# Experts' scatters that add into a row per token, on one core: the shared result is stored first, and the last stage loads one row per token

## The reference, cut to what matters

```python
ys = _geglu(xf @ Ws1 + bs1) @ Ws2 + bs2
logits = (xf @ Wr + br) / TAU
top_val, top_idx = jax.lax.top_k(logits, 2)
top_w = jax.nn.softmax(top_val, axis=-1)
...
yE = jnp.einsum('enh,ehd->end', act, We2) + be2[:, None, :]
yr = jnp.einsum('end,ne->nd', yE, w)
return (ys + yr).reshape(B, T, Dm)
...
x = x + _layernorm(_L0_ffn_ref(_layernorm(x, axis=-1), ...), axis=-1)
```

## Time and profile before

| what | value |
|---|---|
| median of 3 runs | 1189.19 us (1187.93 to 1189.62) |
| span of the profiled execution (its own time is given as this span alone) | 1189.8 us |
| PE, PEld busy over the span | 87%, 50% |
| DVE, ACT, POOL busy over the span | 70%, 63%, 53% |
| granted TensorE clock, mean | 0.957 |

### The profile page before, as it was taken

One profiled execution on the slowest core, in us unless ns is written; L12 is line 12 of the kernel. 1 busy time (PEld: TensorE's weight loads), 2 busy tenths in 40 slices (PEclk: granted clock), 3 DMA queues, 4 the chain that ended last, 5 costly groups with the idle time before them and its releaser, 6 DMA issues. The chain is left out here.

```text
span 1189.8 us, 31490 instructions
## 1 busy us (share of the span) xinstructions
PE 1035.2 (87%) x8446; PEld 597.5 (50%) x8446; DVE 833.9 (70%) x2411; ACT 746.2 (63%) x1311; POOL 631.6 (53%) x1184
## 2 busy tenths in 40 slices
PE   4689998898899898998777999866999999999875
PEld 3543333333333333332245665535888888888732
DVE  7587777777777777776768898532666666666737
ACT  4677767777767767775655566413666666666716
POOL 3246666666666666664422777771444444444344
PEclk9799999999999999998996899878999999999988
DMA  8313333333332333333243111112222222221166
GB/s 222 86 56 97 94 94 94 105 92 90 90 107 86 97 93 100 94 98 104 81 127 130 54 55 55 55 55 71 65 60 62 64 61 64 64 65 51 46 220 211
DMA packets 135606, 107.47 MB, mean 90 GB/s; under 512 B 32203, under 2 KB 127874, under 8 KB 135538
## 3 DMA queue, kind: packets, MB, share of 16 engines
q1 hardware_dynamic: 124722, 87.45, 26.1%
q0 software_dynamic: 8544, 17.78, 4.2%
q10 hardware_dynamic: 2272, 1.45, 0.4%
HBM read 55.96 MB, written 50.69 MB: 90 GB/s over the span
## 5 line engine op out<-in xcount | busy, mean ns | idle before, releaser
L1536 DVE TENSOR_REDUCE maxima<-ps 128x8 f32<-128x1024 f32 x320 | 384.3, 1222 | 125.4 <-PE ps L1159 111.1
L911 ACT ACTIVATE pT_area<-ps 128x1024 f32<-128x1024 f32 x320 | 327.7, 1026 | 143.6 <-PE ps L1190 143.0
L699 POOL TENSOR_SCALAR_AFFINE_SELECT pT_area<-pT_area 128x256 f32<-128x256 f32 (+1 forms) x448 | 190.8, 440 | 109.3 <-ACT pT_area L911 107.4
L801 POOL DMA_INDIRECT ys_dram<-quad_area,place_cur x139 | 133.1, 957 | 192.5 <-issue 136.6
L1231 PE MATMUL ps<-pT_area,quad_area 128*32 128x512 f32 (+3 forms) x2048 | 190.6, 446 | 0.0
L791 POOL DMA_INDIRECT xs_dram<-quad_area,idx_cur x128 | 123.0, 961 | 77.6 <-issue 75.2
L1190 PE MATMUL ps<-quad_area 64*128 64x512 bf16 (+3 forms) x1024 | 124.9, 301 | 37.3 <-DVE maxima L1536 34.7
L1398 PE MATMUL ps<-quad_area 128*128 128x256 f32 (+1 forms) x456 | 129.8, 367 | 6.3 <-issue 4.5
L1399 PE MATMUL ps<-quad_area 128*128 128x256 f32 (+1 forms) x456 | 128.3, 363 | 0.0
L1159 PE MATMUL ps<-quad_area 61*128 61x128 bf16 (+2 forms) x1792 | 126.4, 243 | 0.0
L1019 ACT ACTIVATE xnT<-ps,be_cur 128x256 f32<-128x256 f32 (+1 forms) x228 | 94.6, 448 | 47.6 <-PE ps L1399 47.3
(11 more groups left out here) (237 smaller groups left out, 1593.0 us busy)
## 6 DMA issues: line engine op xcount, KB each, us to landing
qk_dram<-split_area SPq DMA_DIRECT2D x192, 128.0 KB, 2.3
quad_area<-qk_dram SPq DMA_DIRECT2D x256, 96.0 KB, 2.3
row_area<-xs_dram SPq DMA_DIRECT2D x63, 132.0 KB, 2.1
pT_area<-ys_dram SPq DMA_DIRECT2D x16, 512.0 KB, 5.3
pT_area<-in_L_ffn_We SPq DMA_DIRECT2D x12, 384.0 KB, 6.1
out_dram<-pT_area SPq DMA_DIRECT2D x7, 512.0 KB, 2.9
xs_dram<-row_area SPq DMA_DIRECT2D x5, 528.0 KB, 4.2
split_area<-in_L_ffn_We SPq DMA_DIRECT2D x12, 192.0 KB, 3.6
```

Source lines behind the costliest of these rows:

```text
L699: return pool.affine_select(out=blocks, in_=blocks, compare_op=ALU.is_ge, fill=0.0, base=0, pattern=[[0, count], [1, P]], channel_multipli ...
L801: pool.indirect_dma_start(ys_dram, at, ys[:, ns % 2, h, :], None).then_inc(s_yst[ns % 2], 16)
L911: act.activation(pT[:, gs % 2, n, :], ps[:, bank:bank + 2, :].rearrange("p a b -> p (a b)"), ACT.Exp).then_inc(s_exp, 1)
L1536: dve.tensor_reduce(to, ps[:, bank:bank + 2, :].rearrange("p a (j k) -> p a j k", k=P), AX, ALU.max).then_inc(s_mxf, 1)
```

## The change

- `ys_dram` has one row per token (and 256 spare rows) in place of two. Token rows lie by partition, `(p t)`, so that a partition's rows are contiguous.
- SyncE stores the shared result of each of the 16 batches into these rows (`store_shared`, 16 DMAs of 256 KB, semaphore `s_yin`): 12 before `pad`, 4 behind the loads of the first three expert tiles. A DMA of zeros fills the spare rows.
- GpSimd waits for these once, ahead of the expert stage. Its scatters then add to the row (`compute_op=ALU.add`). Since two experts add to the same row, it waits ahead of each tile's scatters until those of the tile before have landed (`stored(ns - 3, n - 3)`).
- The place number is a token's row for both experts: VectorE copies it (`tensor_copy`) where it added `second` before. Blank rows all go to the 256 spare rows.
- In the last stage SyncE issues 8 loads of 512 KB, one per pair, all at once, into `summed`, which is the area of `v_all`. TensorE's products and GpSimd's adds are gone; VectorE takes the statistics from `summed`, ScalarE scales it in place, VectorE adds the residual in place and SyncE stores it, by half pairs, in 16 DMAs. The waits for a free buffer are gone.

```diff
+            def store_shared(b):
+                sp.wait_ge(s_ysum, b + 1)
+                sp.dma_start(ys_rows[:, NT * b:NT * b + NT], tiles4(ysum, b)).then_inc(s_yin, 16)
+            for b in range(B - 4):
+                store_shared(b)
...
             for j in range(3):
                 load_rows(j, j, firsts[j])
+            for b in range(B - 4, B):
+                store_shared(b)
...
-            for n in range(3):
-                pick(n)
-            for n in range(PAIRS + 2):
-                if n + 3 < PAIRS:
-                    sp.wait_ge(s_sum, n + 1)
-                    pick(n + 3)
...
+            for n in range(PAIRS):
+                sp.dma_start(pair_of(summed, n), ys_rows[:, R * n:R * n + R]).then_inc(s_pick[n], 16)
...
                 if 0 <= ns - 2:
                     pool.wait_ge(s_wt, 5 * n - 8)
                     wait_apart(pool, s_yesb, n - 1, s_passed)
+                    if ns - 3 >= 0:
+                        wait_apart(pool, s_yst[(ns - 3) % 2], stored(ns - 3, n - 3), s_passed)
                     for h in range(halves(ns - 2)):
                         at = bass.IndirectOffsetOnAxis(ap=place_cur[:, (ns - 2) % 4, h:h + 1], axis=0)
-                        pool.indirect_dma_start(ys_dram, at, ys[:, ns % 2, h, :], None).then_inc(s_yst[ns % 2], 16)
+                        pool.indirect_dma_start(ys_dram, at, ys[:, ns % 2, h, :], None, compute_op=ALU.add).then_inc(s_yst[ns % 2], 16)
...
+            pool.wait_ge(s_yin, 16 * B)
+            pool.wait_ge(s_dump, 16)
             expert_steps(pool, expert_tile)
...
-            for n in range(PAIRS):
-                ge(pe, s_normal, 2 * (n - 3))
...
-                    pe.matmul(ps[:, bank, :], ident[:], shared_y, start=True, stop=False)
...
-                dve.tensor_tensor(place_cur[:, ring, h], xs[:, ring, h, PLACE], second, ALU.add).then_inc(s_wt, 1)
+                dve.tensor_copy(place_cur[:, ring, h], xs[:, ring, h, PLACE]).then_inc(s_wt, 1)
...
-                    dve.wait_ge(s_sum, n + 1)
-                    ge(dve, s_normal, 2 * (n - 2))
+                    dve.wait_ge(s_pick[n], 16)
                     for t in range(R):
-                        last = dve.bn_stats(st2[:, par, t, :], summed(n, t))
+                        last = dve.bn_stats(st2[:, par, t, :], summed[:, R * n + t, :])
```

More of the change, by code:

```diff
@@ L357, in build @@
         s_ye = sem("expert_y_done"); s_yesb = sem("expert_y_ready"); s_yst = [sem(f"ys_stored{n}") for n in range(2)]
-        s_wt = sem("weight_steps"); s_added = sem("picked_added"); s_sum = sem("routed_sums"); s_shift = sem("shift_ready"); s_normal = sem("normalised"); s_pick = [sem(f"rows_picked{n}") for n in range(3)]
+        s_wt = sem("weight_steps"); s_shift = sem("shift_ready"); s_normal = sem("normalised"); s_pick = [sem(f"rows_picked{n}") for n in range(B // 2)]
         s_st3 = sem("stats3"); s_seedC = sem("seedC"); s_newtC = sem("newtonC"); s_fin = sem("final_steps")
@@ L519, in step @@
                     sp.wait_ge(s_zset, i + 1)
+                    if i == 0:
+                        sp.dma_start(ys_dram[TILES * P:].rearrange("(k p) c -> p k c", p=P), blank[:, 0:2, VALUES]).then_inc(s_dump, 16)
                     at = E * ROOM + BLANK_ROWS * i * P
@@ L646, in _ @@
             pool.memset(v_cur[:], 0.0)
[L647 to L651, removed]
+            pool.iota(tag_i[:, 0:BLANKS], pattern=[[0, BLANKS // 2], [P, 2]], base=TILES * P, channel_multiplier=1)
+            pool.iota(tag_i[:, BLANKS:BLANKS + TILES], pattern=[[1, TILES]], base=0, channel_multiplier=TILES)
+            chain(pool.iota(tag_i[:, BLANKS + TILES:], pattern=[[ROOM, E]], base=0, channel_multiplier=0))
+            pool.tensor_copy(tag[:], tag_i[:, BLANKS:BLANKS + TILES])
+            pool.tensor_copy(rooms[:], tag_i[:, BLANKS + TILES:])
             pool.tensor_copy(blank_tag[:], tag_i[:, 0:BLANKS])
@@ L955, in tag_rows @@
                     half = slice(NT * par, NT * par + NT)
-                    for at, t4 in ((PLACE, tags[:, 0, NT * b:NT * b + NT]), (FIRST_W, pair_w[:, 0, half]),
+                    for at, t4 in ((PLACE, tag[:, NT * b:NT * b + NT]), (FIRST_W, pair_w[:, 0, half]),
                                    (SECOND_W, pair_w[:, 1, half]), (SECOND_E, kept_e[:, half])):
@@ L1036, in _ @@
             for n in range(PAIRS):
-                par = n % 2
                 act.wait_ge(s_shift, 2 * n + 2)
-                if n >= 2:
-                    act.wait_ge(s_out[par], 16 * (n // 2))
                 for h in range(2):
                     for t in range(NT * h, NT * h + NT):
-                        last = act.activation(final[:, par, t, :], summed(n, t), ACT.Identity,
-                                              scale=rstd3[:, n % 3, t:t + 1], bias=shift[:, n % 3, t:t + 1])
+                        rows = summed[:, R * n + t, :]
+                        last = act.activation(rows, rows, ACT.Identity, scale=rstd3[:, n % 3, t:t + 1], bias=shift[:, n % 3, t:t + 1])
                     last.then_inc(s_normal, 1)
@@ L1422, in _ @@
             expert_steps(pe, expert_tile)
-            for n in range(PAIRS):
-                ge(pe, s_normal, 2 * (n - 3))
-                for h in range(2):
-                    bank = 2 * (n % 4) + h
-                    tiles = slice(NT * h, NT * h + NT)
-                    shared_y = pair_of(ysum, n)[:, tiles, :]
-                    pe.matmul(ps[:, bank, :], ident[:], shared_y, start=True, stop=False)
-                    if h == 1:
-                        pe.wait_ge(s_pick[n % 3], 32 * (n // 3 + 1))
-                        pe.matmul(ps[:, bank, :], ident[:], picked[:, n % 3, tiles, 1, :], start=False, stop=False)
-                        pe.matmul(ps[:, bank, :], ident[:], picked[:, n % 3, tiles, 0, :], start=False, stop=True)
-                pe.wait_ge(s_added, n + 1)
-                pe.matmul(ps[:, 2 * (n % 4), :], ident[:], picked[:, n % 3, 0:NT, 0, :], start=False, stop=True).then_inc(s_sum, 1)
         @block.vector
@@ L1874, in _ @@
                     dve.tensor_tensor(shift[:, ring], shift[:, ring], pair_of(moved, n - 1), ALU.add).then_inc(s_shift, 1)
-                if n == PAIRS + 1:
+                if n >= 2:
                     for h in range(2):
-                        half, x4 = (t[:, NT * h:NT * h + NT] for t in (final[:, n % 2], pair_of(x_sb, n - 2)))
+                        half, x4 = (t[:, R * (n - 2) + NT * h:R * (n - 2) + NT * h + NT] for t in (summed, x_sb))
                         dve.wait_ge(s_normal, 2 * n - 3 + h)
                         dve.tensor_tensor(half, half, x4, ALU.add).then_inc(s_fin, 1)
-                elif n >= 2:
-                    dve.wait_ge(s_normal, 2 * n - 2)
-                    dve.tensor_tensor(final[:, n % 2], final[:, n % 2], pair_of(x_sb, n - 2), ALU.add).then_inc(s_fin, 2)
 _OUTS = [((16, 512, 128), "float32")]
```

40 lines of the change are left out of this document (12 added, 28 removed).

## The result

The changed kernel takes 1308.12 us (median of four runs, 1304.34 to 1311.38) against 1189.4 us beside it: a ratio of 1.099, 95% interval 1.096 to 1.102. It is slower, as forecast, but by 118.7 us where the forecast had 49.8, and the time lies above the range of 1203 to 1300 us. The profiled execution took 1304.34 us, with a span of 1302.5.

A forecast was written before the change was run, and what follows sets the result against it. TensorE was taken to bound the paired tiles, GpSimd after the change. 833.15 + 63 x 5.06 + 12 x 3.43 = 1193.1, plus 46.1 and 0.4, gave 1239.6, or 1239.0 us against the median; range 1203 to 1300 us.

The forecast's parts named there:

- the round turns from TensorE's into GpSimd's: Paired expert tiles: GpSimd's new wait is not covered, a round taking 4.66 us before the add's price, against TensorE's 4.33.
- the path through place_cur to TensorE: Expert stage: VectorE waits for scatters' landing before overwriting place_cur and ys, delaying the gated multiplies that TensorE needs.
- The form of the sum: GpSimd's paired round: first to second scatter 1.26, landing 2.62, landing to next scatter 0.78, plus 0.4 for the add: 5.06 us.
- The term 0.78: GpSimd, expert stage: 0.78 us from a releaser's end to a scatter's start, claimed to hold for a DMA as releaser too.
- The landing of second scatters, 2.62: Paired tiles: second scatters land after 2.62 us in the mean, since they meet a later tile's row loads.
- rival A: Expert stage: second scatters land in 2.2 us, the add is free, TensorE still bounds; 1183.9 us, faster; chance 0.10.
- The add's price d: Each round's extra for an adding scatter: between 0 and 1.9 us, taken as 0.4; a longer issue would come on top.
- as many bytes again: Adding scatter: reading the old row makes at least another 0.19 us of each engine per scatter.
- Rival C: Expert stage: the add is dear, by a separate round trip or longer GpSimd issue; 1280, 1284.6 or 1353 us; chance 0.18.
- The last stage: After the expert stage: statistics wait for one load (3.9 us), VectorE sets the pace at 4.2 us a pair; gain 9.5 us.
- The stores of the shared result: Before the expert stage: SyncE's stores cost nothing; GpSimd's wait for all 16 is over about 10 us before its first scatter.

## Why the prediction was right in direction and wrong in size

*That the round turns from TensorE's into GpSimd's: shown.* The wait alone makes it 4.53, the DMA named as the releaser, and the path through place_cur to TensorE is the one foretold.

*The form of the sum: shown.* A paired round is first to second scatter, landing, landing to the next scatter. In the changed kernel these are 1.92 + 3.32 + 0.80 = 6.04, and a single round 3.26 + 0.78 = 4.04 against 4.03 measured. The term 0.78 held in both: 1046.68 + 3.27 = 1049.95, and GpSimd's next scatter starts at 1050.72. That it holds behind a DMA the prediction had no row for: the one it cites has VectorE start, 0.02 us after a landing, so this term came right without having been shown.

*The landing of second scatters, 2.62: a little high.* With the wait alone it is 2.46, with plain scatters in the changed kernel 2.33. The row loads that go with the longer ones move once the scatters wait, as rival A said they might; its 2.2 was nearer than the forecast's 2.62 in the second of these kernels, not in the first. Its other condition, a free add, failed.

*The add's price d: the step that failed.* The prediction took d = 0.4 from the queue's engine time, and of a longer issue it said only that "its bound goes in with d": it was put at nothing in the sum. Measured in its own terms, d is 6.04 - 4.66 = 1.38 us for a paired round and 4.03 - 3.03 = 1.00 for a single one. The largest part is the issue: the median scatter takes GpSimd 1560 ns instead of 957. In a paired round that counts twice, once ahead of the second scatter's start (1.92 instead of 1.26) and once within its landing, which counts from the start of the issue. Of the 1.03 us by which a single scatter lands later (2.23 to 3.26), 0.60 is thus issue, if the rest begins when the issue ends, and 0.43 is left; with half the bytes a single scatter's median landing is no shorter, so this rest is not shown to be the time of the data. Queue 0 shows a rest of like size from its side: 0.089 x 1302.5 = 115.9 us of each engine, less 128 plain scatters at 0.19, leaves 0.66 us for each of the 139 that add, 0.47 more than a plain one. The prediction's "as many bytes again" was thus a lower end that held; whether reads and writes of one scatter overlap, as its 0.4 assumed, no run shows. What it mis-sized is above all the issue, the larger half of d, for which the sum had no term. Its row was there to be distrusted: 957 ns is the price of an issue without an add, and nothing in the trace bounded the other.

*Rival C was the case, and the range cut it off.* C named this mechanism, "GpSimd's issue takes longer since there is more to describe", counted twice a paired round, but with 0.3 us where 0.60 was measured. The range left out C above d = 1.2, though the text itself had 1.9 as the bound: the measured 1.38 lies in the part that was dropped.

The Trainium skill, "DMA: Bandwidth & Descriptors", section "Anatomy of one DMA — SWDGE (gpsimd) path", has a fixed 2.0 us and bytes over 436 GB/s; by that, an estimate, a transfer of twice the 64 KB would land 0.15 us later. The adding scatter landed 1.03 us later, and with half the bytes as late, so the runs disagree with it where a DMA adds.

*The last stage: right.* It shortened by 11.1 us where 9.5 less d was forecast. The first statistics start 3.77 us after the load's issue (3.9 forecast), the pace is 3.94 us a pair (4.2), the tail 1302.5 - 1289.89 = 12.6 (13.3); against that the first load is issued 3.25 us after the last scatter's start, in place of 2.29 in before, the add's price once more.

*The stores of the shared result: no cost seen.* The first scatter starts at 829.08. In the kernels that have these stores and no others ahead of it, it starts between 829.08 and 835.18, with 833.15 in before, so 4 us either way is scatter between executions. In the expectations for the two kernels with zeros in the attention stage, on the other hand, the stores were priced far too low; the kernel with 21 such stores starts its expert scatters 26.7 us later, the one with eight 13 to 17 us later.

## What to carry to other kernels

An operation's price matters by where it stands: the same adding scatter costs 0.19 us of a round where only buffers wait for it and 1.5 us where the next one waits for its landing. So before a step goes into a one-by-one chain, measure it by itself, issue and landing apart, and if its price can't be had from a trace, keep the range up to the bound. The chain is there because two neighbouring tiles may add to the same rows. The Trainium skill, "DMA: Bandwidth & Descriptors", section "Rules for kernel authors", has an accumulating DMA wait for an earlier one on the same bytes; no run here added to the same rows without that wait. Two destinations in turn lift the wait between neighbours, but then the sum that was saved at the end comes back.

## What the runs showed of the hardware that was not expected

An indirect scatter of 128 rows that adds takes GpSimd 1560 ns to issue where a plain one takes 957, and, in single tiles, lands after 3.26 us in the mean instead of 2.23. It is cut into more packets: 8544 / 267 = 32 for a plain scatter, (24112 - 128 x 32) / 139 = 144 for an adding one, at the same bytes; with half the bytes in each row the issue, the packets and the median landing stay, but not the engines' time, which falls from 0.66 to (0.074 x 1301.6 - 24.3) / 139 = 0.52 us.
